# Attended values as 32x32 blocks on 16 tiles of the array, turned by VectorE, in a transformer block on one core

## The reference

```python
def _L0_cond_ref(x, timestep_embed, ...):            # one embedding row per sequence
    shift1, scale1, gate1, shift2, scale2, gate2 = jnp.split(ada, 6, axis=-1)
    x1 = _ln(x) * (1.0 + scale1) + shift1
    qkv = (x1 @ qkv_w + qkv_b).reshape(Bc, Tc, 3, H, DH)      # H = 16, DH = 128
    attn = jnp.einsum('bthd,bshd->bhts', q, k) * scale
    attn = jax.nn.softmax(attn, axis=-1)
    attn_out = jnp.einsum('bhts,bshd->bthd', attn, v).reshape(Bc, Tc, INNER)
    attn_out = attn_out @ out_w + out_b
    x = x + gate1 * attn_out
    x2 = _ln(x) * (1.0 + scale2) + shift2
    h = jax.nn.gelu(x2 @ ffn_w1 + ffn_b1, approximate=False)
    return x + gate2 * (h @ ffn_w2 + ffn_b2)

def _L0_ffn_ref(x, w1, g1, w2, g2, w3, g3):          # _linear_bit: int8 rows x ternary weights
    h = jax.nn.silu(_linear_bit(x, w1, g1)) * _linear_bit(x, w2, g2)
    return _linear_bit(h, w3, g3)

x = x + _L0_ffn_ref(_L0_cond_ref(x, ...), ...)
```

## Time and profile before

| | |
|---|---|
| median of 3 runs | 338.66 us (338.62 to 338.73) |
| profiled execution | span 336.9 us, 9816 instructions |
| TensorE busy | 330.3 us (98%), matmuls 4197 |
| VectorE busy | 215.2 us (64%) |
| ScalarE busy | 183.1 us (54%) |
| GpSimd busy | 121.5 us (36%) |
| TensorE clock granted | 9 tenths or more in all 40 slices |
| HBM read, written | 22.68 MB, 1.11 MB |

### The profile page before, as it was taken

The page is one execution under the profiler, slowest core; times in us unless marked ns, Lnnn a source line. Parts: engine busy times, 40 slices in busy tenths (PEclk is TensorE's granted clock), DMA queues, the critical chain, the costliest instruction groups (busy, mean ns, idle before and its releaser), DMA issues.

```text
span 336.9 us, 9816 instructions
## 1 busy us (share of the span) xinstructions
PE 330.3 (98%) x4197; PEld 299.6 (89%) x4197; DVE 215.2 (64%) x420; ACT 183.1 (54%) x356; POOL 121.5 (36%) x107
## 2 busy tenths in 40 slices
PE   8999999999999999999999999999999999999986
PEld 8989989899998989899898999889998889998765
DVE  3846966815858953505167236679565789886896
ACT  3754654454426365356423816478535576628794
POOL 1373405000934762555311413032620123304591
PEclk9999999999999999999999999999999999999999
DMA  7984930500045540110010000100010200200011
GB/s 241 369 283 175 299 129 2 151 8 2 2 146 170 158 158 34 64 33 2 3 56 11 2 20 14 43 24 2 2 62 2 64 3 2 64 2 2 0 33 62
DMA packets 20834, 24.41 MB, mean 72 GB/s; under 512 B 1780, under 2 KB 18328, under 8 KB 20792
## 3 DMA queue, kind: packets, MB, share of 16 engines
q1 hardware_dynamic: 20416, 23.50, 21.5%
q10 hardware_dynamic: 376, 0.30, 0.3%
HBM read 22.68 MB, written 1.11 MB: 71 GB/s over the span
## 4 chain that ended last, share of the span: by engine, by line
PE 88%; DVE 6%; ACT 4%; issue 1%; POOL 0%; DVEq 0%; ACTq 0%
PE proj_banks L564 40%; PE out_bank L564 15%; PE att_banks L657 8%; PE wide_banks L564 4%; PE turn_bank L564 3%; PE proj_banks L627 3%; PE wide_banks L848 2%; PE att_banks L564 2%; PE att_banks L892 1%; PE wide_banks L657 1%; ACT work L1855 1%; PE att_banks L848 1%; PE wide_banks L731 1%; ACT L1714 1%; DVE hamax L1466 1%
## 5 line engine op out<-in xcount | busy, mean ns | idle before, releaser
L1721 ACT ACTIVATE q_t<-proj_banks,bias_cols 128x256 f32<-128x256 f32 x64 | 30.6, 477 | 54.3 <-PE proj_banks L564 54.3
L564 PE MATMUL proj_banks<-x_hi,w_hi 128*128 128x256 f32 x252 | 52.8, 291 | 0.0
L564 PE MATMUL proj_banks<-x_lo,w_hi 128*128 128x256 f32 x252 | 50.7, 283 | 0.0
L564 PE MATMUL proj_banks<-x_hi,w_lo 128*128 128x256 f32 x252 | 50.7, 283 | 0.0
L1233 DVE TENSOR_TENSOR v_sb<-proj_banks,bv_row 128x512 f32<-128x512 f32 x32 | 21.7, 685 | 32.3 <-PE wide_banks L657 30.6
L564 PEld LDWEIGHTS proj_banks<-x_hi,w_hi 128*128 128x128 f32 x252 | 39.6, 191 | 1.5 <-issue 0.4
L564 PEld LDWEIGHTS proj_banks<-x_hi,w_lo 128*128 128x128 f32 x252 | 39.2, 191 | 0.0
L564 PEld LDWEIGHTS proj_banks<-x_lo,w_hi 128*128 128x128 f32 x252 | 39.2, 191 | 0.0
L657 PEld LDWEIGHTS att_banks<-probs_t,v_sb 32*128 32x128 f32 x512 | 29.8, 186 | 5.5 <-issue 5.4
L657 PE MATMUL att_banks<-probs_t,v_sb 32*128 32x32 f32 x512 | 31.6, 272 | 0.0
L1721 ACT ACTIVATE k_t<-proj_banks,bias_cols 128x256 f32<-128x256 f32 x64 | 30.2, 471 | 0.0
(11 more groups left out here) (324 smaller groups left out, 776.6 us busy)
## 6 DMA issues: line engine op xcount, KB each, us to landing
stage<-in_L_cond_qkv_w SPq DMA_DIRECT2D x16, 256.0 KB, 4.5
gate<-gate_rows_scratch SPq DMA_DIRECT2D x48, 64.0 KB, 2.4
stage<-in_L_cond_qkv_w SPq DMA_DIRECT2D x4, 512.0 KB, 5.0
stage<-in_L_cond_out_w SPq DMA_DIRECT2D x4, 512.0 KB, 4.3
work<-in_L_ffn_w SPq DMA_DIRECT2D x2, 1024.0 KB, 10.0
xin<-in_x SPq DMA_DIRECT2D x7, 256.0 KB, 2.9
bv_row<-in_L_cond_qkv_b SPq DMA_DIRECT2D x4, 256.0 KB, 5.7
work<-in_L_cond_ada_w SPq DMA_DIRECT2D x1, 1024.0 KB, 9.7
```

The source lines that it names most:

```text
L564: mm = pe.matmul(dst, l, r, start=start and i == 0, stop=stop and i == len(seq) - 1)
L1721: act.activation(dst[:, h, :], proj_bank[h % 2][:, s * QT:(s + 1) * QT], ACT.Identity, bias=bias_cols[:, c:c + 1]).then_inc(qk_kept, 1)
```

## The change

`attend` takes its operands the other way round: the 32x32 block of `probs_t` is now stationary, and the 32 rows of `v_sb` (128 head dimensions of one head) move. Each product uses one 32x32 tile of the array: row group j, column group h, 16 tiles in all. The result lies as 32 tokens by 128 dimensions, on the 32 partitions of its head. VectorE turns the 32x32 blocks out of PSUM into a new SBUF tile `at_raw` (`at_turn`, two transposes of 128x512 per unit), which shares its place with `at_lo`; ScalarE's `at_high` copies from `at_raw`, and `at_low` subtracts in place: on VectorE for units 0 to 6 and 15, on GpSimd for units 7 to 14. The rows of the output weights are rearranged to fit (four DMAs per group instead of one). Those who waited for `at_lo_made` because of the PSUM banks now wait for `at_turned`. The orders are moved on all engines:

- TensorE: `attend(u-1)` stands before the last `qk_unit` in the first pass, behind the second in units 8, 10, 12 and 14, before `v_unit(u, 0)` in units 9, 11, 13 and 15; `out_proj(u-1, 0)` of units 9, 11 and 13 behind `ffn1` and `hq_turn`.
- VectorE: the two `at_turn` before `keep_v`; in units 12 and 14 behind `quantise_weigh`; `x2_low` one place later.
- ScalarE: `at_high` of the odd units behind `x2_high`.
- GpSimd: `at_low(7)` behind `low_v(3)`, `at_low(8)` behind `low_wo(3)`; for q = 1 to 3 `at_low(8+2q-1)` at the head of the round and `at_low(8+2q)` behind `ffn_bias`.

```diff
-    wo_d = out_w.rearrange("(h p) c -> p h c", p=P)
+    wo_d = out_w.rearrange("(g h d e) c -> g h e d c", g=NG, h=HG, d=HG)
...
+        at_raw = at("at_raw", [P, 2, HG, P], F32, floor.where["at_lo"])
...
-                sp.dma_start(wo_stage, wo_d[:, g * HG:(g + 1) * HG, :]).then_inc(wo_in, 16)
+                for h in range(HG):
+                    sp.dma_start(wo_stage[h * TB:(h + 1) * TB, :, :], wo_d[g, h]).then_inc(wo_in, 16)
...
-                    pe.wait_ge(at_lo_made, 2 * u)
+                    pe.wait_ge(at_turned, 2 * u)
...
-                            dst = att_pairs(u)[j // 2][:, j % 2, (t * HG + h) * TB:(t * HG + h + 1) * TB]
-                            mm = pe.matmul(dst, v_sb[r, t, h * P:(h + 1) * P], probs_t[r, t * HG + h, :],
+                            dst = att_pairs(u)[j // 2][h * TB:(h + 1) * TB, j % 2, t * P:(t + 1) * P]
+                            mm = pe.matmul(dst, probs_t[r, t * HG + h, :], v_sb[r, t, h * P:(h + 1) * P],
                                            start=True, stop=True)
...
-                pe.wait_ge(at_hi_made, 2 * u + 2)
+                pe.wait_ge(at_hi_made, 2 * u + t + 1)
...
-                           late=("lhsT", (at_lo_made, 2 * u + 2)) if t == 0 else None).then_inc(out_mm, 1)
+                           late=("lhsT", (at_lo_made, 2 * u + t + 1))).then_inc(out_mm, 1)
...
             for q in range(NQ):
                 u, b, a = HALF + 2 * q, q - 1, q - 2
-                for h in range(HG):
-                    qk_unit(u, h)
+                qk_unit(u, 0)
+                qk_unit(u, 1)
+                attend(u - 1)
+                qk_unit(u, 2)
+                qk_unit(u, 3)
                 v_unit(u, 0)
-                attend(u - 1)
                 if a >= 0:
                     q_turn(a, 0)
                 v_unit(u, 1)
...
-            def at_low(u, p):
-                dve.wait_ge(at_hi_made, 2 * u + p + 1)
-                dve.tensor_tensor(att_to(at_lo, p), att_from(u, p), att_to(at_hi, p).bitcast(F32),
-                                  ALU.subtract).then_inc(at_lo_made, 1)
+            def at_turn(u, p):
+                dve.wait_ge(attended, 2 * u + 2)
+                dve.transpose(att_to(p), att_from(u, p)).then_inc(at_turned, 1)
+
+            def at_low(u, t):
+                dve.wait_ge(at_hi_made, 2 * u + t + 1)
+                dve.tensor_tensor(at_lo[:, t], at_raw[:, t], at_hi[:, t].bitcast(F32), ALU.subtract).then_inc(at_lo_made, 1)
 
             def attention_tail(u):
                 if u > 0:
+                    for p in range(2):
+                        at_turn(u - 1, p)
                     keep_v(u, 0)
...
                     weighed = [quantise_weigh(a, t) for t in range(2)]
+                for p in range(2):
+                    at_turn(u - 1, p)
+                if a >= 0:
                     for t in range(2):
                         ffn_after(weighed[t])
                         quantise_round(a, t, quantise_amax(t))
...
-            def at_high(u, p):
-                act.wait_ge(attended, 2 * u + 2)
-                act.copy(att_to(at_hi, p), att_from(u, p)).then_inc(at_hi_made, 1)
+            def at_high(u, t):
+                act.wait_ge(at_turned, 2 * u + 2)
+                act.copy(at_hi[:, t], at_raw[:, t]).then_inc(at_hi_made, 1)
...
+            def at_low(u):
+                for t in range(2):
+                    pool.wait_ge(at_hi_made, 2 * u + t + 1)
+                    pool.tensor_tensor(at_lo[:, t], at_raw[:, t], at_hi[:, t].bitcast(F32), ALU.subtract).then_inc(at_lo_made, 1)
...
             low_wo(2)
             low_v(3)
+            at_low(HALF - 1)
             accumulate(3)
             low_wo(3)
+            at_low(HALF)
             low_f2()
 
 
             for q in range(1, NQ):
                 b, a = q - 1, q - 2
+                at_low(HALF + 2 * q - 1)
                 if a >= 0:
                     for t in range(2):
                         rms_of(a, t)
                 gate_bias(b)
                 x2_rstd(b)
                 ffn_bias(b)
+                at_low(HALF + 2 * q)
```

More of the change, by code:

```diff
@@ L342, in adaln_bitffn @@
         attended = sem("attended")
+        at_turned = sem("at_turned")
         at_hi_made = sem("at_hi_made")
@@ L725, in tern_turn @@
                     pe.wait_ge(tern_kept, 2 * p)
-                pe.wait_ge(at_lo_made, 2 * TERN_UNITS[p])
+                pe.wait_ge(at_turned, 2 * TERN_UNITS[p])
                 for b in range(2):
@@ L746, in end_x2_turn @@
                 pe.wait_ge(xn2_ready, 2 * b + t + 1)
-                pe.wait_ge(at_lo_made, 2 * NU)
+                pe.wait_ge(at_turned, 2 * NU)
                 for k in range(KD):
@@ L872, in hq_turn @@
                 else:
-                    pe.wait_ge(at_lo_made, 2 * (HALF + 2 * b + 5))
+                    pe.wait_ge(at_turned, 2 * (HALF + 2 * b + 5))
                 for m in range(MT):
@@ L916, in _ @@
                     qk_unit(u, 0)
-                for h in range(1 if u > 0 else HG // HALVES, HG):
+                for h in range(1 if u > 0 else HG // HALVES, HG - 1):
                     qk_unit(u, h)
+                if u >= 1:
+                    attend(u - 1)
+                qk_unit(u, HG - 1)
                 if u in (2, 4):
@@ L972, in _ @@
                 qk_unit(u, 3)
+                attend(u - 1)
                 v_unit(u, 0)
-                attend(u - 1)
                 v_unit(u, 1)
                 score(u)
-                out_proj(u - 1, 0)
+                if u == NU - 1:
+                    out_proj(u - 1, 0)
                 if u < NU - 1:
                     if b >= 0:
-                        pe.wait_ge(at_lo_made, 2 * u)
+                        pe.wait_ge(at_turned, 2 * u)
                         ffn1(b, range(MT))
@@ L998, in _ @@
             out_proj(NU - 2, 1)
-            pe.wait_ge(at_lo_made, 2 * (NU - 1))
+            pe.wait_ge(at_turned, 2 * (NU - 1))
             ffn1(a, range(0, 2))
@@ L1571, in _ @@
                     split_v(3)
-                if a < 0:
-                    keep_v(u, 0)
-                for p in range(2):
-                    at_low(u - 1, p)
-                if a >= 0:
-                    keep_v(u, 0)
+                keep_v(u, 0)
                 keep_v(u, 1)
@@ L1600, in _ @@
                     weighed = hidden_weigh(a, 0)
+                for p in range(2):
+                    at_turn(u - 1, p)
                 keep_v(u, 0)
-                for p in range(2):
-                    at_low(u - 1, p)
-                keep_v(u, 1)
                 if b >= 0:
                     x2_low(b, b + 1)
+                keep_v(u, 1)
                 softmax_shift(u)
@@ L1616, in _ @@
                     for p in range(2):
-                        at_low(u, p)
+                        at_turn(u, p)
+                    for t in range(2):
+                        at_low(u, t)
                 if a >= 0:
@@ L1922, in _ @@
                     load_table(ACT.Silu)
-                for p in range(2):
-                    at_high(u - 1, p)
+                for t in range(2):
+                    at_high(u - 1, t)
                 if a >= 0:
@@ L1964, in _ @@
                     if u == NU - 1:
-                        for p in range(2):
-                            at_high(u, p)
+                        for t in range(2):
+                            at_high(u, t)
                     gelu(b, 1)
```

16 lines of the change are left out of this document (8 added, 8 removed).

## The result

The changed kernel takes 361.1 us (359.8 to 363.5), the kernel before 338.7: a ratio of 1.067 (1.063 to 1.071), 22.4 us slower. The forecast was slower, at 351.7.

What follows compares the result with a forecast made beforehand. TensorE, busy 98% of the span, was taken as the bound. Attend's -19.2 us and waits of 7.4, 3.4, 1.5, 12.2 and 4.7 gave +10.0; with +3 for the clock, 338.7 became 351.7 us (66%: 345 to 359; 80%: 338 to 366).

Steps and rivals of the forecast that it cites:

- The long waits: Units 12 and 14: TensorE waits 6.1 us each before q_turn, as rms_of queues behind at_low on GpSimd; +12.2 us.
- unit 8's 3.4: Unit 8: TensorE waits for GpSimd's at_low, behind low_wo(2) and low_v(3), before out_proj(7,0)'s third product; +3.4 us.
- q_turn 14.1 us into the unit: Unit 12: rounding on VectorE, which q_turn needs, ends 14.1 us in; TensorE would be there at 8.0.
- The small waits: TensorE waits: units 1 to 7 +7.4 us, units 9 and 11 +1.5, units 13, 15 and the tail +4.7.
- I take 0.7 us: Attend in each of 16 units: 0.7 us instead of 1.92, 16 tiles side by side; -19.2 us.
- It is prefetched by units: 0: Output weights in four DMAs instead of one: prefetched by units and read no earlier, so 0 us.
- The clock term: Half pace behind the two 6 us waits: half of 2.9 us taken for each, +3 us.
- left to a rival: Rival: the clock falls in all three long waits for the full time, 8.7 us instead of 3; 357 us, 8%.
- that of the tiles not running side by side: Rival: attend stays at 1.9 us, the -19.2 us gain goes; 371 us, 10%.
- that of the small waits melting away: Rival: small waits in units 2 to 7, 9, 11, 13, 15 (13.6 us) vanish; 335 us, faster, 10%.
- Waits half as long: Rival: TensorE's waits are half the forecast length; 339.3 to 345 us, 4%.

Runs made afterwards that it cites:

- Experiments 1: Changed kernel with GpSimd's at_low(9), (11), (13) behind rms_of instead of ahead of it: 345.7 us, ratio to before 1.020.
- (2): Changed kernel with GpSimd's at_low(7) ahead of low_wo(2) and low_v(3): 355.6 us.
- Experiment 6: Changed kernel with at_low(odd), at_low(7) and first output-weight DMAs moved, plus four order changes on TensorE and VectorE against small waits: 330.1 us, ratio 0.975.
- (7): Changed kernel with attend's loops turned, so four matmuls in a row use the same 32 rows: 359.9 us, single run.
- (8): Changed kernel with one semaphore step of 2 at attend's last matmul instead of one behind each tile of 128 tokens: 361.8 us, single run.
- 9: Experiment 6's kernel with attend of units 1 to 8, 10, 12 and 14 in two halves around a qk_unit: 335.4 us.
- (3): Changed kernel with the first group's four output-weight DMAs issued behind the second group's v weights: 359.4 us.
- (12): Changed kernel with 24 idle 128x128 products on TensorE before q_turn(0, 0) and q_turn(1, 0): 357.3 us.
- 5: Changed kernel with at_low(odd) behind rms_of, at_low(7) ahead of low_wo(2) and first output-weight DMAs later: 338.3 us, ratio 1.000.
- experiment 10: Experiment 6's kernel with at_low of units 7 to 14 on VectorE behind keep_v(u, 1), none on GpSimd: 340.2 us, ratio 1.003.

## Why the prediction was right, and where it was short

It said slower by 13 us; it was 22.4, inside the 338 to 366 but above the 345 to 359 to which it gave 66%. The mechanism and its places were right; three sizes were not.

- **The long waits** of units 12 and 14 (6.1 us each) measured 6.05 both times, unit 8's 3.4 measured 3.5 (gaps between TensorE's starts, less the usual 0.3). Experiments 1 and 2 show the causes. The step "q_turn 14.1 us into the unit" came 0.3 later in the trace.
- **The small waits.** 7.4 us were forecast for units 1 to 7; the same sum over the gaps in the changed kernel's trace gives 7.1, the largest, 1.7 us each, before score in units 2 and 4 as described. Units 9 and 11: 1.5 forecast, 1.6 measured; units 13, 15 and the tail: 4.7 forecast, 4.5 measured. All waits: 29.2 forecast, 28.8 measured. Experiment 6 took 8.2 us off by orders alone, where the small waits were 13.2: most of them came from the orders, and VectorE had room for the turns.
- **"I take 0.7 us" for attend failed.** It is 1.00, so the gain is 14.7 us and not 19.2: 4.5 of the miss. I counted waves of the array (four passes of 0.12 us and the drain) for all 64 records. Half of them go that way; the other half follow each other singly or in pairs, at some 17 ns. Neither the order of tiles (7) nor the semaphore (8) sets that; 9 shows that a series of 32 doesn't have it. What sets it stays open. That the fetching of instructions does is argued, not shown; a rival that no run separates from it is that the second 32 records load new weights into the same 16 tiles which the first 32 have just used.
- **"It is prefetched by units: 0" for the output weights failed.** That holds for the later groups. The first group's DMA stands in the SP queue at the start, ahead of loads that the first unit waits for. It cost 1.7 us in the median (3), and in the profiled execution about 4.
- **The clock term** was taken as half of 2.9 us for two waits, 3 us. It was 3.8 for these (12) and 2.0 for unit 8 (2), which I had left to a rival: 2.8 short. The single price varies by about 1 us from wait to wait and from run to run, as said under 2 and 12; the sum uses the medians.

-14.7 + 28.8 + 1.7 + 5.8 = 21.6, against 22.4 measured; 0.8 is not assigned. Of the rivals, that of the tiles not running side by side is out (16 records start within 0.10 us); that of the small waits melting away is out too, by the sum above. The clock did fall behind all three waits, at two thirds of that rival's price. In "Waits half as long" the sum was wrong: half of 29.2 us taken from 351.7 gives 337, faster than before, and not 339.3 to 345. It did not come about.

## What to carry to other kernels

In a program of hand-written queues, ask for every step that is moved onto another engine what now stands behind it there, and when its own input comes: in two rounds a pair of subtractions (2.5 us) ahead of small operations of 0.8 us each cost 15 us together, because its input stood behind all the keeps and a table load on ScalarE. A faster stage whose result takes one more step needs that much more room before its consumer, and the queues around it must be sorted anew; done so, the same tiles gave 8.5 us instead of costing 22.4. Idle time of TensorE of 3.5 to 6 us cost about 2 us (1.4 to 2.8) more than its length here.

## What was not expected of the hardware

- A series of 64 short records on 16 tiles has two speeds: 32 records in 0.24 us, the next 32 in 0.68.
- Behind a wait of 3.5 us the clock fell as it did behind one of 6, and that cost as much (2.0 against 1.9 us). In the changed kernel's profile it fell behind the 2.67 us at the start as well.
- One DMA of 512 KB, cut into four by partitions (32 each), took 0.82 us per issue in the queue instead of 0.57, and delayed the start by between nothing and 3.7 us. Moving it brought the spread of the runs down to 0.5 us in experiment 3, but in 5 it was 3.0, so that the spread has another source too stays open.
- VectorE's subtraction of two SBUF operands (at_lo from at_raw) has a mean of 0.85 us, but 13 of its 16 take 0.68 to 0.69, as the one from PSUM does. The three slow ones run while GpSimd works, and the pair of unit 5 takes 3.70 us:

```profile
98.32 3.70 DVE L1271 TENSOR_TENSOR at_lo<-at_raw,at_hi 128x512 fp32r<-128x512 f32 x2
```

```profile
94.22 7.26 POOL L2096 TENSOR_TENSOR f_lo<-stage,f_hi 128x1024 fp32r<-128x1024 f32 x2
```

The pair ends at 102.02, half a microsecond after GpSimd's work has ended (101.48). In the kernel before, the subtraction from PSUM in the same unit took its usual 0.69 beside the same work of GpSimd (89.12 to 95.90):

```profile
93.13 0.69 DVE L1259 TENSOR_TENSOR at_lo<-att_banks,at_hi 128x512 fp32r<-128x512 f32 x1 [0.72 <-ACT at_hi L1730]
```

So taking the operand from SBUF instead of PSUM made this step of VectorE wait for GpSimd, which the prediction has nowhere. In the changed kernel it delays the low part of one unit (TensorE waits 0.4 us for it); in experiment 10 it is one of the causes.
